# A joined loop and a new drain in an attention and triangle kernel: P's transposes in free banks, VectorE on half of P, step 7's u ahead of step 6's output, layer-two weights by masks

## The reference

```python
def layer0(z):                       # attention over the 16 sequences at every grid position
    zn = layernorm(z) * ln_w + ln_b
    q, k, v = (zn @ W).reshape(n, l, l, 8, 16)        # for Wq, Wk, Wv
    g = sigmoid(zn @ Wg + bg)
    att = softmax(einsum('iabhc,jabhc->ijabh', q, k) / 4, axis=1)
    o = einsum('ijabh,jabhc->iabhc', att, v) * g
    return o @ Wo + bo

def layer1(z):                       # triangle product over one grid axis
    zn = sparse_norm(z, alpha_in, beta_in)            # mean and variance of the whole tensor
    a = sigmoid(lin(zn, W_ga, b_ga)) * lin(zn, W_la, b_la)
    b = sigmoid(lin(zn, W_gb, b_gb)) * lin(zn, W_lb, b_lb)
    k = einsum('bitc,bjtc->bijc', a, b)
    kn = sparse_norm(k, alpha_o, beta_o)
    return sigmoid(lin(zn, W_go, b_go)) * lin(kn, W_lo, b_lo)

x = x + layer0(gn(x))
x = x + layer1(gn(x))
```

## Time and profile before

| | us |
|---|---|
| runs (3) | 306.76, 306.80, 307.67; median 306.8 |
| profiled execution | 306.67, its span 304.7 |
| mean granted TensorE clock | 0.947 |

### The profile page before, as it was taken

The page is one execution under the profiler, slowest core; times in us unless marked ns, Lnnn a source line. Parts: engine busy times, 40 slices in busy tenths (PEclk is TensorE's granted clock), DMA queues, the critical chain, the costliest instruction groups (busy, mean ns, idle before and its releaser), DMA issues.

```text
span 304.7 us, 8156 instructions
## 1 busy us (share of the span) xinstructions
PE 247.1 (81%) x3339; PEld 146.0 (48%) x3344; DVE 238.6 (78%) x447; ACT 217.2 (71%) x399; POOL 197.5 (65%) x175
## 2 busy tenths in 40 slices
PE   3964873889899799799799799797777489999983
PEld 1452351466456456456356356355452245565562
DVE  3997879688999999899897887886677874543694
ACT  4757776679889779779779789778271857774390
POOL 8907788789998988988967925607438694000053
PEclk9995798799999999999999999999799589999999
DMA  7301123014032023032022023300000006554216
GB/s 240 76 0 43 29 61 81 0 44 98 1 87 55 2 72 71 2 84 58 2 78 64 0 68 74 70 4 1 2 2 0 1 6 133 147 152 126 69 56 220
DMA packets 32576, 18.14 MB, mean 60 GB/s; under 512 B 21084, under 2 KB 29596, under 8 KB 32540
## 3 DMA queue, kind: packets, MB, share of 16 engines
q1 hardware_dynamic: 32540, 17.63, 21.6%
HBM read 8.18 MB, written 5.77 MB: 46 GB/s over the span
## 4 chain that ended last, share of the span: by engine, by line
DVE 39%; PE 32%; ACT 10%; issue 6%; POOL 6%; DMA 4%; SPq 3%; DVEq 0%; ACTq 0%
PE PS L1197 29%; DVE t_sb L940 5%; DVE nmax L955 5%; DVE S_sb L959 4%; DVE og L915 4%; DVE sums L876 4%; SPq L339 2%; DVE Z L1187 2%; ACT u_sb L623 2%; POOL PP L449 2%; DVE PP L920 2%; ACT t_sb L637 2%; DVE xT L905 2%; DMA x_tok<-in_x 1%; POOL zc L487 1%
## 5 line engine op out<-in xcount | busy, mean ns | idle before, releaser
L1197 PE MATMUL PS<-znT,A_bd 128*128 128x512 f16 x192 | 49.8, 407 | 14.0 <-DVE t_sb L940 12.1
L443 POOL TENSOR_TENSOR S_sb<-S_sb,rden 128x512 f32<-128x512 f32 x32 | 35.4, 1130 | 24.4 <-DVE rden L895 24.4
L940 DVE TENSOR_TENSOR t_sb<-PS,t_sb 128x512 f16<-128x512 f32 x64 | 41.0, 685 | 11.1 <-ACT t_sb L637 11.1
L637 ACT CAST t_sb<-PS 128x512 f16<-128x512 f32 x64 | 36.3, 612 | 16.6 <-PE PS L1197 15.5
L449 POOL TENSOR_TENSOR PP<-S_sb,PP 128x512 f16<-128x512 f32 x32 | 36.5, 1158 | 7.0 <-ACT PP L631 7.0
L1197 PEld LDWEIGHTS PS<-znT,A_bd 128*128 128x128 f16 x192 | 17.9, 103 | 44.8 <-DVE t_sb L940 24.3
L1197 PEld LDWEIGHTS PS<-PP,Z 128*128 128x128 f16 x512 | 29.3, 114 | 13.0 <-issue 12.1
L623 ACT COPY u_sb<-PS 128x512 f32<-128x512 f32 x64 | 32.7, 615 | 1.8 <-PE PS L1197 1.8
L1197 PE MATMUL PS<-zbd,t_sb 128*128 128x64 f16 x768 | 26.6, 193 | 7.4 <-DVE t_sb L940 4.8
L1197 PE MATMUL PS<-PP,Z 128*128 128x128 f16 x512 | 31.4, 220 | 0.7 <-DVE S_sb L959 0.7
L1197 PEld LDWEIGHTS PS<-zbd,t_sb 128*128 128x128 f16 x768 | 23.8, 98 | 15.7 <-DVE S_sb L959 7.0
(11 more groups left out here) (207 smaller groups left out, 521.0 us busy)
## 6 DMA issues: line engine op xcount, KB each, us to landing
Z<-zn_dram SPq DMA_DIRECT2D x64, 64.0 KB, 2.8
x_tok<-in_x SPq DMA_DIRECT2D x4, 512.0 KB, 5.7
zn_dram<-zn_tok SPq DMA_DIRECT2D x8, 256.0 KB, 2.0
zbd<-znT SPq DMA_DIRECT2D x32, 64.0 KB, 2.0
out_x<-u_sb SPq DMA_DIRECT2D x4, 512.0 KB, 3.2
k_dram<-og SPq DMA_DIRECT2D x3, 512.0 KB, 4.1
th<-k_dram SPq DMA_DIRECT2D x12, 128.0 KB, 3.0
PP<-u_sb SPq DMA_DIRECT2D x8, 128.0 KB, 2.4
```

What stands on the lines that cost most here:

```text
L443: nc.gpsimd.tensor_tensor(P, P, bcast(rden[:, 32 * k:32 * k + 32], 2, N), ALU.mult).then_inc(p_nrm, 1)
L637: nc.scalar.copy(t_sb[:, HI, :, h], bank_tg(h)[:, :].rearrange("p (q i) -> p q i", i=N)).then_inc(t_hi, 1)
L940: nc.vector.tensor_tensor(t_sb[:, LO, :, h], bank_tg(h)[:, :].rearrange("p (q i) -> p q i", i=N), t_sb[:, HI, :, h], ALU.subtract).then_in ...
L1197: return nc.tensor.matmul(o, l, r, start=start, stop=stop)
```

## The change

In the loop: DVE adds x1 first, then the sums; `dve_stats` goes behind the third t_lo; the gates of o are spread over the fourth to sixth t_lo; PT's part 0 is copied by ACT; ve goes from DVE to POOL; ACT's `act_ln_high` goes behind the first exp; u's parts go into pairs of banks (5, 6, 3, 4) and are copied in 4 copies of 1024 columns. Period 1 delays the second sums and the centring, and splits p_low. Periods 8 and 9 are replaced by a drain of their own: P's transposes of step 7 go to banks 0, 1, 2, 0; DVE normalises parts 2 and 3 and makes one low half; PE does u of step 7 before out of step 6. The weights of layer 1 are made on POOL, over all partitions, with masks. POOL waits for both halves of DVE's group 0 before its z1_norm of group 1.

```diff
+        PS34 = ctx.enter_context(nc.psum_tensor("PS34", [128, 1024], f32))
+        PS56 = ctx.enter_context(nc.psum_tensor("PS56", [128, 1024], f32))
-        bank_u = lambda i: PS[(5, 3, 4, 6)[i % 4]]
+        bank_u = lambda s, i: PS[((5, 6, 3, 4) if s < NS - 1 else (3, 4, 5, 6))[i % 4]]
+        pair_u = lambda s, i: (PS56, PS34)[(i + (s == NS - 1)) % 2]
+        bank_b7 = lambda i: PS[(0, 1, 2, 0)[i]]
...
         def pool_ln_rstd(pool, j, par):
-            pool.wait_ge(ln_v, LV * (j + 1))
+            pool.wait_ge(ln_v, ln_base(j + 1))
+            nc.gpsimd.tensor_scalar(ln_ve[:, par], ln_var[:, par], 1.0 / D, EPS, ALU.mult, ALU.add).then_inc(ln_e, 1)
+            pool.wait_ge(ln_e, j)
...
+            pool_period(pool, NS - 1, 1)
+            pool_norm(pool, NS - 1, (0, 1))
+            p_low(pool, nc.gpsimd, NS - 1, (0, 1, 3))
+            pool_sqx(pool, NS - 3)
+            pool_weights2(pool)
+            pool_sqx(pool, NS - 2)
...
             pool.wait_ge(g2_ok, 10)
+            pool.wait_ge(z1_m[0], 8)
             z1_norm(pool, nc.gpsimd, 1, z1_m[1])
...
+        def act_drain(act):
+            m = NS - 1
+            act_u_copies(act, m - 1, range(4))
+            for k in range(4):
...
+                act.wait_ge(pt_mm, 4 * (m - 1) + k + 1)
+                nc.scalar.copy(P2[:, 8 * k:8 * k + 8, HI], ...
+            for k in (0, 2):
+                act.wait_ge(pt_mm, 4 * m + k + 1)
+                nc.scalar.copy(PT[:, 8 * k:8 * k + 8] ...
+            act_u_copies(act, m, range(4))
...
             if tail:
...
+                PT_copy(0)
                 PT_copy(1)
+            exps((0,))
             if LN:
                 act_ln_high(act, j + 1, 1 - par, half + par)
...
+        def dve_drain(dve):
+            m = NS - 1
...
+            dve_x1(dve, m - 2)
+            dve_sums(dve, m, 0)
+            dve_reciprocal(dve, m, 0)
+            dve_sums(dve, m, 1)
+            dve_reciprocal(dve, m, 1)
+            dve.wait_ge(p_rec, 2 * m + 2)
+            for k in (2, 3):
+                P = S_sb[:, 8 * k:8 * k + 8].rearrange("p q a n -> p (q a) n")
+                nc.vector.tensor_tensor(P, P, bcast(rden[:, 32 * k:32 * k + 32], 2, N), ALU.mult).then_inc(p_nrm_d, 1)
+            dve_stats(dve, m - 2)
+            dve.wait_ge(p_hi, 4 * m + 3)
+            nc.vector.tensor_tensor(P2[:, 16:24, LO], ...
+            dve_gate_o(dve, m - 1, (0, 1))
+            PT_copy(1)
+            dve_gate_o(dve, m - 1, (2, 3))
+            PT_copy(3)
+            dve_stats_sq(dve, m - 2)
+            dve_biases2(dve)
+            dve_x1(dve, m - 1)
+            dve_stats(dve, m - 1)
+            dve_gate_o(dve, m, range(A2))
+            dve_stats_sq(dve, m - 1)
...
+            if stats:
+                dve_x1(dve, s - 1)
             if tail:
                 dve_sums(dve, m, 0)
                 dve_reciprocal(dve, m, 0)
...
+            for h in range(H):
+                if h == 3:
+                    if j == 1:
+                        dve_sums(dve, m, 1)
+                        dve_reciprocal(dve, m, 1)
+                    if stats:
+                        dve_stats(dve, s - 1)
+                    if B:
+                        gate_o((0, 1))
+                if h in (4, 5) and B:
+                    gate_o((h - 2,))
...
+        def pe_drain(pe):
+            s = NS - 2
+            pe_u(pe, s, s % 2, s // 2, range(8))
+            pe_o(pe, s)
+            pe_PT_last(pe)
+            pe_u(pe, s + 1, (s + 1) % 2, (s + 1) // 2, range(8))
+            pe_out(pe, s)
+            pe_o(pe, s + 1)
+            pe_out(pe, s + 1)
```

More of the change, by code:

```diff
@@ L459, in pool_period @@
             LN = j + 1 < NS
-            if LN:
+            if LN and j != 2:
                 pool_ln_rstd(pool, j + 1, 1 - par)
@@ L656, in act_period @@
             if B:
-                u_copies(range(4))
-            if A and not early:
+                act_u_copies(act, s, (0, 1))
+            if not early:
                 act_znT(act, j)
             if B:
-                u_copies(range(4, 8))
+                act_u_copies(act, s, (2, 3))
             if early:
@@ L906, in dve_x1, with dve_gate_o @@
                                            op0=ALU.add, op1=ALU.add).then_inc(x1_ok, 1)
-        def dve_period(dve, j, par, tail=True, B=True, A=True, stats=True):
+        def dve_gate_o(dve, s, ks):
+            for k in ks:
+                dve.wait_ge(o_mm, HP * s + k + 1)
+                dve.wait_ge(g_th, HP * s + k + 1)
+                nc.vector.scalar_tensor_tensor(out=og[:, k], in0=th[:, s % 2, k], scalar=1.0, in1=bank_o(k)[:, :],
+                                               op0=ALU.add, op1=ALU.mult).then_inc(o_ok, 1)
@@ L909, in dve_period @@
+        def dve_period(dve, j, par, tail=True, B=True, stats=True):
             s, m = j - 2, j - 1
             def gate_o(ks):
[L912 to L916 removed]
+                dve_gate_o(dve, s, ks)
@@ L945, in dve_period @@
                     dve_ln_centre(dve, 2, 0)
-            if B and not A:
-                gate_o(range(A2))
-            if tail:
-                PT_copy(0)
-            if j + 2 < NS:
+            if j == 1:
+                dve_ln_centre(dve, j + 2, par)
+            elif j + 2 < NS:
                 dve_ln_rstd(dve, j + 2, par)
-            for k in range(4 if A else 0):
+            for k in range(4):
                 S = bank_s(k)[:, :].rearrange("p (r n) -> p r n", n=N)
@@ L1088, in _ @@
                     dve_period(dve, 2 * it + 3 + i, 1 - i)
-            for j in range(NS - 1, NS + 2):
-                dve_period(dve, j, j % 2, tail=j <= NS, A=j < NS)
+            dve_period(dve, NS - 1, 1)
+            dve_drain(dve)
             dve_x1(dve, NS - 1)
@@ L1263, in pe_PT, with pe_PT_last @@
                 if k >= 2:
-                    pe.wait_ge(pt_ok[k % 2], 2 * s + 1)
+                    wait_PT(pe, s, k - 2)
                 for q in range(8 * k, 8 * k + 8):
                     last = nc.tensor.transpose(bank_b(k)[:, :].bitcast(f16)[:, 128 * (q % 8):128 * (q % 8) + 128],
+                                               P2[:, q].rearrange("p k m -> p (k m)"), ident16[:, :])
+                last.then_inc(pt_mm, 1)
+        def pe_PT_last(pe):
+            m = NS - 1
+            pe.wait_ge(g_th, HP * NS)
+            for k in range(4):
+                if k == 2:
+                    pe.wait_ge(p_lo_d, 1)
+                else:
+                    pe.wait_ge(p_lo, 4 * m + (1, 2, 0, 3)[k])
+                if k == 3:
+                    wait_PT(pe, m, 0)
+                for q in range(8 * k, 8 * k + 8):
+                    last = nc.tensor.transpose(bank_b7(k)[:, :].bitcast(f16)[:, 128 * (q % 8):128 * (q % 8) + 128],
                                                P2[:, q].rearrange("p k m -> p (k m)"), ident16[:, :])
@@ L1401, in _ @@
                     pe_period(pe, 2 * it + 3 + i, 1 - i, it + i)
-            for j in range(NS - 1, NS + 2):
-                pe_period(pe, j, j % 2, j // 2 - 1, A=j < NS)
+            pe_period(pe, NS - 1, 1, NS // 2 - 2)
+            pe_drain(pe)
             def bias1(i):
```

245 lines of the change are left out of this document (129 added, 116 removed).

## The result

The changed kernel takes 302.73 us (median of 4 runs, 300.29 to 302.79), the kernel before 307.24 beside it (306.76 to 308.01): ratio 0.9866, 95% interval 0.9821 to 0.9910. By the ratio that is 1.34%. It is 4.5 us off the median beside it and 4.1 us off the 306.8 of the forecast's base, where 6.0 was forecast. The profiled execution took 302.79 us with a span of 301.0.

A forecast was written before the change was run, and what follows sets the result against it. No single bound: DVE is nearest to full, but the loop step is a ring through three engines. Head -2.1, loop -1.0, drain -4.1 and norm +1.2 give -6.0: 300.7 us, range 297.0 to 304.5.

The forecast's parts named there:

- Head: Step 1 up to T(2), the start of step 2's scores: 80.5 instead of 82.7, -2.1 us, bounds -4.5 and 0.
- Most of this is given back: Head: of T(1) at 55.9 instead of 60.4, most is lost by T(2), as POOL still works one after another.
- Loop: Steps 2 to 7, from scores to scores: 22.75 instead of 23.15 for steps 3 to 5; -1.0 in all, bounds +1.5 and -6.
- Here the gain of PE is lost: Loop step: o ready at 14.45, before 14.86, but DVE's stats before the gates leave them at 17.15 against 17.19.
- DVE was the bound: Rival, chance 0.1: the loop closes at DVE's work, steps 21.2 to 21.9, 1.0 a step more over four steps: 296.7 us.
- the forecast's own sign of being wrong: Wrong if scores are 23 or more apart, a pair copy exceeds 1.2, or x1-to-end growth falls outside 0.5 to 2 us.
- Drain: From step 7's scores to its x1: 30.2 instead of 34.32, -4.1 us, bounds -5.2 and -2.5.
- cover of POOL: Drain: POOL's mask weights, square, clears and bias rows end at 34.2, its layer-two pow is wanted at 35; 0.8 to spare.
- Norm: Layer-two norm: POOL waits for both DVE halves, its first four end at 245.4 instead of 242.1; +1.2, bounds -0.5 and +2.5.
- rival in which the wait is paid back: Layer-two norm, chance 0.1: DVE's and POOL's four each shrink running alone, +1.2 becomes -0.5, 299.0 us.
- likeliest case: Whole kernel: the forecast of 300.7 us itself, chance 0.45, by itself 298.5 to 302.5.
- the drain gains, the norm gives it back: Rival, chance 0.1: POOL's pow is late in the drain and the norm costs its 2.5: 302.0 to 304 us.

The follow-up runs named there:

- e11_period2: From e5_both: in period 2 ScalarE's cast moved behind the first two tanh; 296.99 us, ratio 0.9701 to the kernel before.
- e5_both: Changed kernel without POOL's layer-two norm wait, and with ScalarE's zn_tok cast ahead of the first exp in periods 3 to 6; 295.13 us, ratio 0.9639.
- e9_step1_order: Changed kernel with VectorE in step 1 again centring and doing both sums and reciprocals ahead of t's low halves; 306.14 us, ratio 1.0013.
- e10_28_small: Changed kernel with 28 small VectorE copies (32x32) added in the drain, into a tile nothing reads; 302.41 us, ratio 0.9892.

## Why the prediction was right in sign, and where its sum was off

**Head.** T(2) was forecast at 80.5 and is 79.90; T(1) at 55.9 and is 56.32. The hole fell as worked out (0.89 and 1.34 for "about 1"). T(0) to T(3) is the fair measure, as what is gained before T(2) and lost behind it moves with TensorE's clock: forecast -1.8 (-2.1 and +0.3), measured -1.56 (66.17 to 64.61), and -1.8 to -2.3 in the other profiles with that code. So this term was sized right. "Most of this is given back" through POOL's queue fits the trace: from 58.8 us to T(3) GpSimd waits only 1.25 and 1.18, both for ScalarE's cast, and its low halves of step 2's P start 61.3 us behind T(0), 61.4 before, though TensorE was ahead by 4.6 at T(1). e11_period2 shows the same by experiment: with TensorE's hole gone, it waits for those low halves. TensorE's wait of 1.44 before u's second half, where before had 0.69 in the middle of 16 and 16, was not forecast; its share and that of ScalarE's later cast were not separated. The cast moved either way alone gives none of T(1) to T(3) back (49.86 and 48.31).

**Loop.** Steps were forecast at 22.75 and are 22.47 to 22.61; TensorE's gate matmuls at T + 4.75 are at T + 4.77, and the pair copy, put at 0.95, takes 1.93 for two. But the reason was wrong. "Here the gain of PE is lost" named VectorE's stats between low half and gates; with the stats where they are, e5_both runs at 21.85, and the gate matmuls come at T + 4.16. What held the steps was the place of ScalarE's cast, and by two ways. One is the stall of TensorE behind it, 0.56 us, which the forecast had seen (4.75 for 4.2) and let VectorE's queue hide. From T(5) to T(7), where GpSimd has idle time ahead of its normalisation (2.12 and 5.38), it goes through to the next T: with the cast behind the tanh these steps are 21.84 for 22.47. The other is GpSimd, of which the forecast said "it keeps 2 us": from T(3) to T(5) it waits for nothing but the cast, 1.41 us a step, and with the cast later still, 2.53, the steps are 23.56. The cast ahead of the exponential removes both at once (GpSimd's wait falls to 0.28), so which of the two ended last from T(3) to T(5) isn't shown. The rival "DVE was the bound" gave steps of 21.2 to 21.9; the loop lands there once the cast is out of the way, with TensorE and GpSimd as full as VectorE, so its mechanism isn't shown by that. Step 2 to 3, forecast at +0.3, is +1.75 in this profile and -0.1 to +1.5 in others with the same code; it was also the one step of the loop that met the forecast's own sign of being wrong, scores 23 or more apart.

**Drain.** -4.1 forecast, -3.53 measured, inside its bounds. P's transposes start at T + 15.16 (forecast 15.2), u of step 7 at 17.78 (17.4), o of step 7 at 24.00 (23.35), x1 at 30.79 (30.2). The 0.6 comes in between the transposes and o, where TensorE waits 0.42 for POOL's low halves and u takes 4.37 with ScalarE's copies. The forecast put out, between u and o, at 0.9 on the path; it didn't price the other order, and taking u first is worth 2.05 against it. The cover of POOL held: its pow waited 0.39 for VectorE, not the other way round. The third that contention was to add to the norms of P shows on VectorE, 1.61 for two where 0.65 each was put, and not on GpSimd, 2.08 for two.

**Norm.** This is the mis-sized term: +1.2 with a bound of 2.5, measured +3.48. POOL's queue was forecast well: its first four were to end 13.4 us behind x1 and end at 13.7, and they were to slip by 3.3 where ScalarE's cast behind them slips by 2.6 between the kernel without and with the wait. What failed is the absorption: "group 2 slips by about 1.7 only" (its cast slips by 2.0, from 15.7 to 17.7 behind x1) and the products' lag were to leave +1.2, but the triangle slips by 3.6, more than either cast. The rest fits TensorE's clock, which behind the holes of the wait was at its lower level for longer: twelve matmuls that take 0.83 us at full clock took 1.46 at two places and 1.17 at a third, and without the wait 1.29 at one. No run moves the clock by itself, so this share is argued. The rival in which the wait is paid back (-0.5) is refuted by both runs of the wait.

```profile
238.47 1.46 PE L1283 MATMUL PS<-W_p,t_sb 64*128 64x256 f16 x12
...
245.15 1.46 PE L1283 MATMUL PS<-W_p,t_sb 64*128 64x256 f16 x12
...
247.21 0.83 PE L1283 MATMUL PS<-W_p,t_sb 64*128 64x256 f16 x12
```

**Sum.** By the profile -3.7, by the medians -4.5, forecast -6.0. The norm is 2.3 of the miss, the drain 0.6, the later start 0.5 and T(0) to T(3) 0.2; a better loop (0.8) and last stretch (0.5) go against it. That the rest cancels, and the norm's 2.3 is the whole miss of the profile, is luck. The start is no part of the change: T(0) lies between 38.3 and 39.9 in all profiles here. The range held the time; the likeliest case's own range, 298.5 to 302.5, just missed it, and the time lies in that of "the drain gains, the norm gives it back" (302.0 to 304). Of that rival the dear norm came true, the late pow did not. Of the forecast's own conditions of being wrong one more was met: the distance from x1 of step 7 to the end grew by 3.0 (72.73 to 75.72), more than the 2 it allowed.

## What to carry to other kernels

Contention between two engines is a price per operation (here 0.7 to 1.1 us for four, on either side); a wait that avoids it costs the whole first engine's work to everybody queued behind the second: compare the two before adding the wait. In a queue that is served in order, ask of every moved operation when its input comes in the worst period, not in the steady one: the cast was cheap ahead of the exponential from period 3 on and dear in period 2. Parts of a serial tail can be worth together less than the sum of what each costs when undone (here 3.5 for 6.5), so measure the whole as well. And when a run undoes one engine's order, look whether another engine's new order still leans on it: e9_step1_order gave GpSimd a wait of 4.57 that neither kernel has.

## What the runs showed of the hardware

GpSimd's four 128x256 operations take 4.11 us beside VectorE's norm, 3.44 beside VectorE's low half and smaller work, and 3.04 with no norm and no low half of VectorE beside them; VectorE's four 128x128 take 2.15 beside GpSimd's and 1.44 without. The Trainium skill, GPSIMD Engine Reference (Specifications), says that GpSimd's SBUF interfaces are shared with VectorE, with contention for VectorE instructions of two SBUF inputs or in a 2-port mode; the trace agrees that they contend, and shows that both sides pay, a third of POOL's time and half of VectorE's. VectorE's norm has one SBUF tensor as input; in which mode it ran no run here shows.

TensorE's clock. From 230 to 238 us TensorE was granted 0.50, the lower level of 1.2 GHz, in the changed kernel and in the one without the wait, around an idle time of 3.62 and 3.73 us ahead of the first W_p matmuls. The table by stages of what follows, columns as in the earlier trace rows, changed kernel first, then without the wait:

```profile
238.00:242.00 4.00, 2.32 (x15) 0.84 (x13) 1.65 (x3) 2.15 (x5) 4.00 (x6) 0.75 0.00 0
242.00:246.00 4.00, 3.24 (x25) 1.42 (x27) 2.37 (x11) 1.60 (x3) 4.00 (x6) 0.68 0.02 4
```

```profile
238.00:242.00 4.00, 3.74 (x37) 1.72 (x34) 2.47 (x13) 2.83 (x7) 4.00 (x6) 0.95 0.01 4
242.00:246.00 4.00, 3.69 (x41) 1.84 (x41) 2.31 (x12) 2.72 (x7) 3.27 (x3) 1.00 0.60 131
```

With the holes of the wait the granted clock came back late (0.75, then 0.68); without them it was 0.95 and then full. The stretch is also uneven with the wait: x1 to the triangle is 26.49 to 28.41 us in the nine profiles that have it and 23.08 to 23.25 in the four without it. In the longest, e10_28_small, the granted clock was 0.65, 0.78 and 0.50 in the three stretches of 4 us from 234 to 246 us.
